# Cross-attention and mixture-of-experts layer: a finer order of the first weight products, and the once-a-batch jobs moved to the ends of groups

## Time and profile before

| | us |
|---|---|
| median of 3 runs (range) | 3330.06 (3328.31 to 3333.57) |
| the profiled execution: own time | 3335.48 |
| its span | 3333.5 |
| PE busy | 3287.3 (99%) |
| DVE busy | 2401.6 (72%) |
| ACT busy | 1936.7 (58%) |
| POOL busy | 1061.6 (32%) |

### The profile page before, as it was taken

How to read it: one execution, slowest core, us unless ns; L and a number is a source line. 1 busy time by engine, 2 the same in 40 slices (tenths; PEclk the granted TensorE clock), 3 DMA queues, 4 the chain that set the end, 5 groups by cost and what they waited for, 6 DMA issues and landing times.

```text
span 3333.5 us, 50432 instructions
## 1 busy us (share of the span) xinstructions
PE 3287.3 (99%) x15589; PEld 2619.0 (79%) x15589; DVE 2401.6 (72%) x4954; ACT 1936.7 (58%) x2239; POOL 1061.6 (32%) x724
## 2 busy tenths in 40 slices
PE   7999999999999999999999999999999999999999
PEld 6777777777777777877777777777777777777887
DVE  5777777777777777777777777777777777777655
ACT  4566556665556565656555656555565556655554
POOL 4222232222332223322223222233222332225555
PEclk9999999999999999999999999999999999999999
DMA  2000000000000000000000000000000000010000
GB/s 90 1 16 1 17 1 10 7 1 17 1 16 1 17 1 16 1 1 17 1 16 1 17 1 16 1 16 2 1 16 1 17 1 16 1 45 4 7 7 10
DMA packets 8682, 35.98 MB, mean 11 GB/s; under 512 B 1657, under 2 KB 2306, under 8 KB 8130
## 3 DMA queue, kind: packets, MB, share of 16 engines
q1 hardware_dynamic: 8386, 32.29, 3.1%
HBM read 29.92 MB, written 2.10 MB: 10 GB/s over the span
## 4 chain that ended last, share of the span: by engine, by line
issue 71%; POOL 18%; PE 9%; DVE 1%; POOLq 0%; ACT 0%; DMA 0%; DVEq 0%; ACTq 0%
POOL p_lo L390 12%; POOL cT_lo L379 2%; PE st L625 2%; POOL v_lo L381 2%; PE st L626 2%; PE st L627 2%; POOL cT_hi L371 1%; POOL v_hi L372 1%; PE op L625 1%; PE op L627 1%; PE op L626 1%; PE side L672 1%; POOL rstd L309 1%; DVE gu_mul L1118 0%; POOLq L389 0%
## 5 line engine op out<-in xcount | busy, mean ns | idle before, releaser
L755 ACT ACTIVATE p_full<-st 128x1024 f32<-128x1024 f32 (+1 forms) x832 | 855.4, 1028 | 1164.6 <-PE st L516 1160.2
L1027 DVE TENSOR_REDUCE m_part<-side 128x1 f32<-128x402 f32 x2048 | 1094.5, 571 | 544.8 <-PE side L460 544.8
L390 POOL TENSOR_TENSOR p_lo<-p_full,p_hi 128x1024 fp32r<-128x1024 f32 x256 | 649.5, 2537 | 2097.1 <-ACT p_hi L758 2097.1
L758 ACT ACTIVATE p_hi<-st 128x1024 fp32r<-128x1024 f32 (+1 forms) x832 | 850.7, 1023 | 0.0
L1015 DVE TENSOR_TENSOR p_lo<-p_full,p_hi 128x1024 fp32r<-128x1024 f32 (+1 forms) x576 | 700.3, 1216 | 141.4 <-ACT p_hi L758 117.9
L460 PE MATMUL side<-cT_hi,qT_hi 96*128 96x402 f32 x2048 | 563.1, 346 | 0.0
L510 PE MATMUL st<-qT_hi,cT_hi 97*128 97x512 f32 (+1 forms) x1668 | 539.9, 405 | 2.9 <-DMA qT_hi<-m_row 2.9
L524 PE MATMUL op<-p_hi,v_hi 128*97 128x512 f32 (+1 forms) x1664 | 527.6, 398 | 6.0 <-DVE p_lo L1015 6.0
L513 PE MATMUL st<-qT_lo,cT_hi 96*128 96x512 f32 (+1 forms) x1668 | 528.0, 397 | 0.0
L516 PE MATMUL st<-qT_hi,cT_lo 96*128 96x512 f32 (+1 forms) x1668 | 523.6, 395 | 0.0
L527 PE MATMUL op<-p_lo,v_hi 128*97 128x512 f32 (+1 forms) x1664 | 519.5, 393 | 0.0
(11 more groups left out here) (146 smaller groups left out, 2636.4 us busy)
## 6 DMA issues: line engine op xcount, KB each, us to landing
keys_nat<-in_ctx_keys SPq DMA_DIRECT2D x18, 624.0 KB, 5.7
keys_tur<-in_ctx_turned SPq DMA_DIRECT2D x18, 603.0 KB, 4.8
out_x<-x SPq DMA_DIRECT2D x8, 256.0 KB, 2.0
x<-in_x SPq DMA_DIRECT2D x1, 1920.0 KB, 12.1
w_rest<-in_moe_w SPq DMA_DIRECT2D x1, 1152.0 KB, 7.2
qT_hi<-m_row SPq DMA_DIRECT2D x65, 4.0 KB
w_first<-in_moe_w SPq DMA_DIRECT2D x1, 960.0 KB, 4.7
aw<-in_attn_w SPq DMA_DIRECT2D x2, 448.0 KB, 5.3
```

The lines of the kernel that those rows point to most:

```text
L390: pool.tensor_tensor(p_lo[:, slot(s), :], p_full[:, s % 2, :], p_hi[:, slot(s), :].bitcast(F32), ALU.subtract).then_inc(s_lo_pool, 1)
L755: act.activation(p_full[0:m, s % 2, :], both(st[0:m, s % 2]), ACT.Exp, scale=SCALE)
L758: act.activation(p_hi[0:m, slot(s), :], both(st[0:m, s % 2]), ACT.Exp, scale=SCALE).then_inc(s_ex, 1)
L1027: dve.tensor_reduce(m_part[:, at:at + 1], where[:, 0:MAXW], AX.X, ALU.max).then_inc(s_drain, 1)
```

## The change

The head: `multiply_weights` does the products of one weight slice c (two heads) a call. Slices 2 to 5 come after pieces 3, 5, 7 and 9, slices 6 and 7 behind all pieces into `st[:,1]`, free once piece 13's maximum is taken. The row of maxima is kept before, not after, DVE's preset of `op`; the wait for all A_lo stands between the first two `scores`; POOL's memset of the ones row of cT_hi and all behind it wait for DVE's first normalising.

The loop: L goes to group 1, N to group 2 and R to group 3, each as the third job of t = 12, behind QQ. Statistics and normalising are done for two tiles at a time: those for L at the ends of groups 3 and 0, those for N at the ends of 0 and 1; POOL makes deviations twice a batch.

```diff
-        x1 = sb(stack, "x1", [P, T + 4, D])
+        x1 = sb(stack, "x1", [P, T + 6, D])
-        EXTRA = {2: {5: "L", 6: "N"}, 3: {5: "R"}}
+        EXTRA = {1: "L", 2: "N", 3: "R"}
         def places(i):
-            return {t: (a, b + EXTRA.get(i, {}).get(t, "")) for t, (a, b) in PLACES.items()}
+            return {t: (a, b + EXTRA.get(i, "") if t == S - 1 else b) for t, (a, b) in PLACES.items()}
...
# POOL, head
-            pool.memset(x1[:, T + 2:T + 4, :], 0.0).then_inc(s_const, 1)
+            pool.memset(x1[:, T + 2:T + 6, :], 0.0).then_inc(s_const, 1)
             pool.wait_ge(s_const, 1)
             deviations(1, slice(0, 2))
             pool.wait_ge(s_rstd, 1)
+            pool.wait_ge(s_xn, 1)
             link(pool.memset(cT_hi[DC:OW, :, :].bitcast(F32), 1.0))
# POOL, group loop
-                            if s == 3 and i == 1:
-                                deviations(bb * 2 + (par + 2), slice(0, 4))
+                            if s == 3 and i < 2:
+                                deviations(bb * 4 + (2 * par + 2 + i), slice(2 * i, 2 * i + 2))
# PE, head: multiply_weights(c, banks) now does one c of the old pair (c = 2n, 2n + 1)
             multiply_weights(0, op)
+            multiply_weights(1, op)
...
-                if u in (2, 6, 8):
-                    n = (2, 6, 8).index(u) + 1
-                    if n == 1:
-                        pe.wait_ge(s_drain, J0_Q + 2)
-                    else:
-                        pe.wait_ge(s_abk, n - 1)
-                    if n < 3:
-                        pe.wait_ge(s_w[n], 16)
-                    multiply_weights(n, side)
+                if u in (3, 5, 7, 9):
+                    c = (u + 1) // 2
+                    if c == 2:
+                        pe.wait_ge(s_drain, J0_Q + 2)
+                        pe.wait_ge(s_w[1], 16)
+                    elif c == 4:
+                        pe.wait_ge(s_abk, 1)
+                        pe.wait_ge(s_w[2], 16)
+                    multiply_weights(c, side)
                 if u == 11:
-                    pe.wait_ge(s_abk, 3)
+                    pe.wait_ge(s_abk, 2)
...
+            pe.wait_ge(s_mxd, NM // 2 - 2)
+            multiply_weights(6, st[:, 1])
+            multiply_weights(7, st[:, 1])
             pe.wait_ge(s_mc, 1)
...
# PE, group loop: the counts that L and N wait for follow the finer s_xn
-                            turn_tokens(where, bb * 2 + (par + 2), 0)
+                            turn_tokens(where, bb * 4 + (2 * par + 2), 0)
...
-            pe.wait_ge(s_Ap, 3)
             pe.wait_ge(s_bo, 16)
             pe.wait_ge(s_rl, 32)
             pe.wait_ge(s_ml, 16)
             scores(0, 0, 0)
+            pe.wait_ge(s_Ap, 3)
             scores(1, 0, 0)
# ACT, head
-            for n in range(1, 4):
+            for n in range(1, 3):
                 keep_products(n, side).then_inc(s_abk, 1)
             for k in range(2):
                 queries_hi(bank(J0_Q1 + k), J0_Q1 + k + 1, k, 1)
+            keep_products(3, st[:, 1]).then_inc(s_abk, 1)
# ACT, group loop: the extra job is kept after the loop over s and both queries_hi, not inside it
# DVE, head
             combine_max()
+            keep_max_rows(bank(J0_T), J0_T + 1)
             dve.memset(op[0:OW, :, :], 1.0).then_inc(s_set, 1)
-            keep_max_rows(bank(J0_T), J0_T + 1)
             dve.wait_ge(s_xr, 16)
             dve.wait_ge(s_const, 2)
             carry()
+            token_stats((4, 5), 0)
# DVE, after_jobs of group i
-                    if i in (0, 1):
-                        tiles = [dve.snap(bb * 4 + (2 * par + q)) for q in (4, 5, 0, 1)]
+                    if i != 2:
+                        tiles = [dve.snap(bb * 4 + (2 * par + q)) for q in {0: (4, 5, 0, 1), 1: (0, 1), 3: (6, 7)}[i]]
                     if i == 0:
+                        normalise(tiles[0:2], 0, bb * 4 + (2 * par + 2))
                         dve.wait_ge(s_drain, jobs + (job_at[i]["Y"][-1] + 1))
-                        token_stats(tiles, 0, links)
+                        carry()
+                        token_stats(tiles[2:4], 2, links)
                     elif i == 1:
-                        normalise(tiles, 0, bb * 2 + (par + 2))
+                        normalise(tiles, 2, bb * 4 + (2 * par + 3))
                         route_groups(links)
...
                     else:
+                        token_stats(tiles, 0, links)
                         route_scores(links)
```

More of the change, by code:

```diff
@@ L397, in _ @@
                                 piece_lo(bb, par, i)
-            deviations(B + 2, slice(2, 4))
+            deviations(2 * B + 3, slice(2, 4))
             after_attention(pool)
@@ L433, in route_logits, with multiply_weights @@
                 mm.then_inc(s_fill, 1)
[L435 to L446, removed]
+            def multiply_weights(c, banks):
+                k = c % 2
+                for j in range(2):
+                    r = slice(j * DH, (j + 1) * DH)
+                    pe.matmul(banks[:, j, k * DC:(k + 1) * DC], aw[r, c, 0:P], aw[r, c, P:P + DC],
+                              start=True, stop=True)
+                for j in range(2):
+                    r = slice(j * DH, (j + 1) * DH)
+                    mm = pe.matmul(banks[0:DC, j, 2 * DC + k * P:2 * DC + (k + 1) * P],
+                                   aw[r, c, P + DC:P + 2 * DC], aw[r, c, P + 2 * DC:448], start=True, stop=True)
                 mm.then_inc(s_ab, 1)
@@ L561, in side_jobs @@
                         elif kind == "L":
-                            turn_tokens(where, bb * 2 + (par + 2), 0)
+                            turn_tokens(where, bb * 4 + (2 * par + 2), 0)
                         elif kind == "N":
-                            turn_tokens(where, bb * 2 + (par + 2), 2)
+                            turn_tokens(where, bb * 4 + (2 * par + 3), 2)
                         elif kind == "R":
@@ L617, in _ @@
             pe.wait_ge(s_drain, JOBS_END + GH - 1)
-            turn_tokens(bank(JOBS_END + GH), B + 2, 2)
+            turn_tokens(bank(JOBS_END + GH), 2 * B + 2, 2)
             pe.wait_ge(s_drain, JOBS_END + GH + 1)
@@ L713, in keep_products @@
                 if n:
-                    act.wait_ge(s_ab, n + 1)
+                    act.wait_ge(s_ab, 2 * n + 2)
                     act.activation(four_heads(A_raw, n), products(banks, slice(0, 2 * DC)), ACT.Copy)
@@ L721, in _ @@
             tokens_hi(bank(J0_X), 0, J0_X + 1)
-            act.wait_ge(s_ab, 1)
+            act.wait_ge(s_ab, 2)
             act.activation(four_heads(A_hi, 0), products(op, slice(0, 2 * DC)), ACT.Copy).then_inc(s_xh, 1)
@@ L764, in body @@
                     exp(s)
[L765 to L775, removed]
                 for k in range(2):
@@ L778, in body @@
                     queries_hi(bank(jobs0 + j), jobs + (j + 1), k, i % 2)
+                extra = EXTRA.get(i)
+                if extra:
+                    j = job_at[i][extra][0]
+                    where, filled = bank(jobs0 + j), jobs + (j + 1)
+                    if extra == "L":
+                        tokens_hi(where, 1 - par, filled)
+                    elif extra == "N":
+                        act.wait_ge(s_fill, filled)
+                        keep_x2(where, bass.ds(bb * (2 * NQ) + par * NQ, NQ))
+                    else:
+                        keep_exponentials(where, filled)
             with act.Fori(0, B // 2) as bb:
@@ L1069, in body @@
                 after_jobs()
-            links_per_turn = 46
+            links_per_turn = 50
             with dve.Fori(0, B // 2) as bb:
@@ L1093, in _ @@
             after_attention(dve)
-            normalise((T, T + 1), 2, B + 2)
+            normalise((T, T + 1), 2, 2 * B + 2)
             for q in range(2):
```

## The result

The changed kernel takes 3386.79 us (median of 5, 3384.65 to 3387.23), the kernel before 3333.25 (5 runs beside it, 3328.31 to 3334.44): ratio 1.0159, 95% interval 1.0148 to 1.0171, 53.5 us slower. The profiled executions differ by 51.8 us in span (3385.3 and 3333.5).

A forecast was written before the change was run, and what follows sets the result against it. PE bounds the loop (busy 2938 of 2957 us). Moved jobs +52.8, back edges -2.5 and head -4.1 sum to +46.2 us, which on 3330.06 gives 3376 us; range 3358 to 3392.

The forecast's parts named there:

- PE is the bound, its waits are paid in full: In the loop PE is busy 2938 of 2957 us; whatever makes it wait is paid in full.
- The wait for the first Q bank: At the ends of groups 1, 2 and 3, PE waits 1.31 us for DVE to drain the bank.
- What is removed: At the jobs' old places in the loop, L and N save 1.19 us and R 0.43, 1.62 a batch.
- DVE's extra work is hidden: At the group ends, DVE's new work, up to +1.4 us, does not exceed PE's new delay and costs nothing.
- The back edges give a little back: At 7 loop back edges PE's wait shrinks by about 0.35 us each, -2.5 us in all.
- The head: Before the loop: start, maxima and row of maxima together gain 4.1 us, bounds -0.5 and -6.
- Start: In the head, DVE's two normalisings no longer run beside POOL's memset: -2.1 us, bounds 0 and -2.4.
- the maxima: In the head, one weight slice at a time cuts DVE's idle 6.5 us to 4.85: about -1.5, bounds 0 and -3.
- rival 1: ACT or DVE sets the next group's start, so PE only waits earlier, not longer: 3316 us; 6%.
- rival 2: Each of 48 PE waits in the loop drops the clock, losing 2.6 us each, 125 in all: 3501 us; 4%.
- rival 3: DVE's work at group 3's ends is 1 us or more longer, costing at back edges and inside the loop: 3387; 8%.
- rival 4: PE's wait at the group ends is shorter, about N's 0.65 us: 32 us less, 3344; 4%.

The follow-up runs named there:

- run behind single Ms: Changed kernel with L, N and R each moved behind the single M of step 5 of its new group: 3323.02 us, ratio 0.997 to the kernel before.
- last run: On top of the run behind single Ms, DVE's two-tile statistics (step 4) and sigmoid and bias (step 6) inside each turn's last group: 3311.5 us, ratio 0.9935.

## Why the prediction was right, and where its sizes were off

- *PE is the bound, its waits are paid in full.* Right: 57.3 us of new waits, less N's 7.8 and the 2.6 at the back edges, are 46.9 us, and the loop's idle time grew by 46.3. The loop is 54.8 us longer (52.93 + 1.88). The other 8 us are PE's busy time: of each new wait 0.16 us (1.37 - 1.21, next point) is not counted as idle, 7.7 us in all. By the stretches, N's old wait had such a part too (some 3.5 us), and the jobs' own instructions cost about as much more at the new place.
- *The wait for the first Q bank.* Right in place, chain and count. As the profile counts it, 1.21 us is idle; from the time at which `weigh(11)` would have begun (QQ's begin at 128.83 and 1.42) to the transposes at 131.62 it is 1.37, where I said 1.31. The term that was small is the lag from DVE's release to PE: 0.13 us, not 0.07. With R at 0.47 instead of 0.43, a batch costs 3.53 us, not 3.30: +3.7 us in all.
- *What is removed*, 1.62 us a batch. The total is as read; its parts are the jobs' own 0.23, 0.25 and 0.4 in the run behind single Ms (0.28, 0.28 and 0.43 read), and the rest, 0.7, is N's wait (0.63 read).
- *DVE's extra work is hidden.* Right: its idle time ahead of `lo(0)` grew behind groups 1, 2 and 3, from 0.50 to 1.81, 0.54 to 1.24 and 1.34 to 1.58 us. *The back edges give a little back.* Right: 6.0 to 3.4 us, 2.5 forecast.
- *The head*, -4.1 forecast, -3.65 at the first scores. Start -2.23 (2.1 forecast), the row -0.55 (0.5), the maxima -0.87 (39.40 - 36.29 - 2.23 = 0.88) where I had 1.5. In this trace that term was too large: I had 4.85 us of DVE's idle time left, and 4.7 + 0.8 are. The gap behind the queries is 2.13 us (2.45 forecast); the four beside the single slices are 0.50, 0.84, 0.84 and 0.84, 3.0 in all, where I had 0.2, 0.6, 0.95 and 0.65, 2.4; and the 0.41 ahead of the first reduces, which is in the 6.5 of before, I had left out of what remains. PE's speed in the head is part of it: in the six other traces with this head the turning of the maxima is at 35.17 to 36.27 instead of 36.29, by which the term would be 0.9 to 2.0, around the 1.5. Another 0.45 went to PE's lower speed behind the first scores. I had left the speed equal in both places, so that the head's sum came within 0.9 us is in part luck.
- *Rivals.* The wait was not given back in the next group (rival 1); the granted clock stayed at 1.00 through the waits (rival 2); DVE was not late (rival 3); the wait was not N's 0.65 (rival 4).

The sum was +46.2, the spans say +51.8 and the medians +53.5. Of the 5.6 us between forecast and span, 3.7 are the lag and R, 0.8 is spread over the loop, 0.9 is the head with its slower start (-3.2 instead of -4.1 at the first mark) and 0.2 the tail.

## What to carry to other kernels

A job's cost on the engine that bounds the kernel is its own instructions plus the time until its buffer is free, and the second part is read at the new place: follow the buffer two jobs back, to the last instruction that frees it, and look at what that engine does first. The end of a group, where the other engines do their last big pieces, was the worst place for these jobs of those tried; the same jobs one `weigh` later on PE cost 54 us less. Work taken from a busy place must be weighed by how often each place occurs and by what stands beside it there: three pieces at steps 6, 8 and 10 of every group 3 cost 1.1 us each time and lost more than the back edges won, while two of them at steps 4 and 6 of each turn's last group cost nothing that shows. Since the steps, the pieces and the groups were changed together, their shares are not known.

## What the hardware showed that was not expected

- In the head of the kernel after PE ran at its lower speed though the granted clock read 1.00: the three-product series of 256 columns are 0.21 us apart at 27.9 to 30.0 us (rows in the run of the head alone) and 0.12 in the loop (first two rows below). In the last run the column did show the lower level in the head, 0.51 over 26 to 30 us (third row), and the same products take the same 0.42 us there. Where it read 1.00 in the head, only the durations tell.

```profile
128.83 0.28 PE L453 MATMUL side<-x_hi,A_hi 128*96 128x256 f32 x1
128.95 0.28 PE L454 MATMUL side<-x_lo,A_hi 128*96 128x256 f32 x1
```
```profile
26.00:30.00 4.00, 4.00 (x17) 3.64 (x17) 1.86 (x3) 1.55 (x3) 4.00 (x3) 0.51 0.00 0
```

- When the speed rose in the head differed between kernels with the same instructions on PE there: the seven with the whole new head have their first scores at 37.79 to 39.02 us and their first mark at 78.67 to 80.43. Some 1.8 us of a 3334 us kernel hang on it, so a gain of that size in a head cannot be read from one trace.
- A short vector instruction on 64 columns took 1.02 us instead of 0.19 beside a subtraction on POOL. What is cheap by its mean is not cheap at every place.
- At the loop's back edge DVE does nothing for 3.0 to 3.6 us, in the eight kernels in which nothing that the profile shows holds it there; what it does in that time stays open. Moving 2 us of its work ahead, to where it idles, took PE's wait away there.
